# A sequence kernel in three stages: part of the second stage's input is loaded and scaled inside the first, and squares move from GpSimd to VectorE

## The reference, cut to what matters

```
q, k, v = x@Wq, x@Wk, x@Wv          # split into 16 heads
q, k    = rmsnorm(q)*qw, rmsnorm(k)*kw
gate    = softplus((k . u_n) / 8)
scores  = q.k/8 - (i-j)*omega_h*gate_j ; causal; softmax
x       = layernorm(x + (attn @ v) @ Wproj)
```

```
h = silu(x@w1' * s1) * (x@w2' * s2)
h = gelu(h@h1' * s3) ; h = gelu(h@h2' * s4)
x = layernorm(x + h@w3' * s5)
```

## Time and profile before

| | us |
|---|---|
| median of 3 runs | 3400.02 |
| lowest and highest run | 3398.07, 3406.59 |
| the profiled execution, its own time | 3401.34 |
| its span, first to last instruction | 3399.6 |
| TensorE busy | 3158.8 (93%) |
| VectorE, ScalarE, GpSimd busy | 1659.2, 1794.1, 1499.9 |
| mean granted TensorE clock | 0.97 of full |

### The profile page before, as it was taken

The page is one execution under the profiler, slowest core; times in us unless marked ns, Lnnn a source line. Parts: engine busy times, 40 slices in busy tenths (PEclk is TensorE's granted clock), DMA queues, the critical chain, the costliest instruction groups (busy, mean ns, idle before and its releaser), DMA issues. The chain is left out here.

```text
span 3399.6 us, 45979 instructions
## 1 busy us (share of the span) xinstructions
PE 3158.8 (93%) x15472; PEld 2456.8 (72%) x15472; DVE 1659.2 (49%) x3920; ACT 1794.1 (53%) x3057; POOL 1499.9 (44%) x1318
## 2 busy tenths in 40 slices
PE   3999999999999999999999999679999999899998
PEld 3667767767767677677677677467777778688887
DVE  6565565566565665655665666142222222232322
ACT  1576676667666766766776777532222222222222
POOL 4476676566666666666766766421111110000000
PEclk6899999999999999999999999889999999899999
DMA  2242332322432422422323323432232221312120
GB/s 76 65 92 49 73 85 46 84 68 50 95 77 61 99 61 51 100 48 67 87 46 81 76 50 85 111 110 87 87 87 87 87 87 38 107 66 75 42 71 19
DMA packets 196539, 249.12 MB, mean 73 GB/s; under 512 B 67280, under 2 KB 95056, under 8 KB 196176
## 3 DMA queue, kind: packets, MB, share of 16 engines
q1 hardware_dynamic: 196304, 246.19, 28.2%
HBM read 84.86 MB, written 43.52 MB: 38 GB/s over the span
## 5 line engine op out<-in xcount | busy, mean ns | idle before, releaser
L385 POOL TENSOR_TENSOR e_lo<-e_all,e_hi 128x512 fp32r<-128x512 f32 (+1 forms) x832 | 1032.1, 1249 | 654.6 <-ACT e_all L627 588.8
L627 ACT ACTIVATE e_all<-ps_s,bias 128x512 f32<-128x512 f32 (+3 forms) x1280 | 788.6, 623 | 168.3 <-PE ps_s L929 80.3
L814 DVE TENSOR_REDUCE maxes<-ps_m 128x1 f32<-128x512 f32 x768 | 521.2, 686 | 371.6 <-PE ps_m L907 368.8
L620 ACT ACTIVATE e_hi<-ps_s,bias 128x512 fp32r<-128x512 f32 (+1 forms) x832 | 560.1, 673 | 228.7 <-PE ps_s L927 134.1
L907 PE MATMUL ps_m<-k_ext,q_max 128*128 128x512 f32 (+3 forms) x1280 | 462.2, 382 | 54.3 <-DVE maxes L814 25.1
L926 PE MATMUL ps_s<-q_twice,k_split 128*128 128x512 f32 (+3 forms) x1280 | 478.0, 373 | 28.3 <-ACT e_all L627 23.3
L927 PE MATMUL ps_s<-q_ext,k_ext 128*128 128x512 f32 (+3 forms) x1280 | 469.9, 367 | 0.0
L960 PE MATMUL ps_v<-e_lo,v_main 128*66 128x512 f32 (+1 forms) x832 | 431.7, 519 | 17.3 <-POOL e_lo L385 17.3
L907 PEld LDWEIGHTS ps_m<-k_ext,q_max 128*128 128x128 f32 x1280 | 245.5, 192 | 202.5 <-DVE maxes L814 59.0
L811 DVE CUSTOM_DVE_ANT_0 ps_m<-ps_m,mask_row 128x128 f32<-128x128 f32 (+3 forms) x512 | 252.5, 496 | 282.3 <-PE ps_m L907 281.9
L949 PE MATMUL ps_v<-e_hi,v_main 128*66 128x512 f32 (+1 forms) x832 | 322.2, 387 | 0.0
(11 more groups left out here) (247 smaller groups left out, 6112.3 us busy)
## 6 DMA issues: line engine op xcount, KB each, us to landing
q_twice<-q_max SPq DMA_DIRECT2D x256, 128.0 KB, 2.3
yt<-y_out SPq DMA_DIRECT2D x128, 130.0 KB
k_ext<-kq_hi SPq DMA_DIRECT2D x128, 128.0 KB, 2.3
q_max<-kq_hi SPq DMA_DIRECT2D x128, 128.0 KB, 2.4
k_split<-kq_hi SPq DMA_DIRECT2D x128, 128.0 KB, 2.4
k_split<-kq_lo SPq DMA_DIRECT2D x128, 128.0 KB, 2.4
q_ext<-kq_lo SPq DMA_DIRECT2D x128, 128.0 KB, 2.4
y_in<-yt SPq DMA_DIRECT2D x128, 128.0 KB, 3.1
```

The costliest lines, as they stand in the source:

```text
L385: on.tensor_tensor(e_lo[:, i % LO_RING, off:QB], e_all[:, u_ % E_RING, off:QB], e_hi[:, i % HI_RING, off:QB].bitcast(F32), ALU.subtract).t ...
L620: nc.scalar.activation(e_hi[:, i % HI_RING, off:QB], ps_s[u_ % 2][:, off:QB], ACT.Exp, bias=by).then_inc(hi_done, 1)
L627: nc.scalar.activation(e_all[:, u_ % E_RING, off:QB], ps_s[u_ % 2][:, off:QB], ACT.Exp, bias=by).then_inc(ex_done, 1)
L814: nc.vector.tensor_reduce(maxes[:, qt, kc:kc + 1], ps_m[m % 2][:, 0:width], AX.X, ALU.max).then_inc(mx_free, 1)
```

## The change

Six edits, all in `attention` and the start of `ffn_up`:

1. A class `Kept` holds what lives in both functions. Its helper `room` gives one place in the on-chip memory (SBUF) to several tensors in turn: `stage` and `y_first` lie where `xt_hi`/`xt_lo` were, `r_first` and `x_tok` in `raw`, `wp_in` in `sq`, `y_hi` in `y_out`. The identity of `attention` is used in `ffn_up` too.
2. Steps are added to the list near its end, with waits on SP that the old tenant is done. SP: `stage` (4 pieces of w1 and w2, 512 KB each, from 3.0 heads before the end), `out weights` (Wproj, 1 MB, 2.55 before), `first y` (16 DMAs, from 2.4), `first r` (16 DMAs, from 1.4), `first x` (0.5). GpSimd: `first scale`, eight multiplications of 128x512, 0.36 to 0.15 heads before the end.
3. Squares: ScalarE's copy to `raw` now sets `pj_raw`; VectorE waits for it, multiplies the PSUM bank by `raw` (128x256: q and k of both heads for one tile of tokens) into `sq`, and only this sets `pj_free`. GpSimd squares no more. The sums are 4 per pair, each of 128x1024, right after every fourth project.
4. The last head's `sums` and `sums out` are taken out of `attention`; SP loads them at the start of `ffn_up`, VectorE takes the reciprocal after `turn_x(0)`, and SP stores it after the eighth piece of weights.
5. In `ffn_up`, `weights(c)` and the first block's y alternate: TensorE does `weights(c)`, `project_y(0, c)` for c = 0 to 7; ScalarE `y_hi`, `w_hi`; VectorE `y_lo`, `w_lo`. GpSimd no longer makes an identity, and scales y from block 1 on.
6. ScalarE loads the table of Silu ahead of `turn_x(0)`.

The diff, cut to its core:

```
+    for i in range(STAGES):
+        at(HEADS - 3.0 + 0.1 * i, "stage", i)
+    at(HEADS - 2.55, "out weights")
+    for c in range(OC):
+        at(HEADS - 2.4 + 0.1 * c, "first y", c)
+        at(HEADS - 1.4 + 0.1 * c, "first r", c)
+        at(HEADS - 0.36 + 0.03 * c, "first scale", c)
+    at(HEADS - 0.5, "first x")
...
-        for i in range(4):
-            at(t0 - 1.44 + 0.05 * i, "square", p, i)
-            at(t0 - 1.38 + 0.05 * i, "sum", p, i)
-            at(t0 - 1.22 + 0.04 * i, "square", p, i + 4)
-            at(t0 - 1.16 + 0.04 * i, "sum", p, i + 4)
+        for i in range(TT // TQ):
+            at(t0 - 1.72 + 0.030 * (TQ * i + 3) + 0.03, "sum", p, i)
...
-    steps += [("sums", HEADS - 1), ("sums out", HEADS - 1)]
...
+                if step[0] == "first scale":          # GpSimd
+                    c = step[1]
+                    if c == 0:
+                        gp.wait_ge(kept.first_load, 16 * 4 * OC)
+                    nc.gpsimd.tensor_tensor(kept.y_first[:, c, :], kept.y_first[:, c, :], kept.r_first[:, c, :], ALU.mult).then_inc(kept.first_scaled, 1)
...
-                    nc.scalar.activation(raw[:, t, :], work_bank(step)[:, 0:WCOLS], ACT.Copy).then_inc(pj_free, 1)
+                    nc.scalar.activation(raw[:, t, :], work_bank(step)[:, 0:WCOLS], ACT.Copy).then_inc(pj_raw, 1)
...
+                if step[0] == "project":              # VectorE
+                    p, t = step[1:]
+                    dve.wait_ge(pj_raw, TT * p + t + 1)
+                    nc.vector.tensor_tensor(sq[:, t % (2 * TQ), :], work_bank(step)[:, 0:CB], raw[:, t, 0:CB], ALU.mult).then_inc(pj_free, 1)
...
             def first_x(i):                           # ffn_up, ScalarE
+                for k in range(2):
+                    act.wait_ge(kept.y_out_done[k], 16 * NQB // 2 * HEADS)
                 for c in range(OC):
                     split_y(i, c)
+                    weights(c)
+                nc.scalar.preload_act_table(ACT.Silu)
                 turn_x(i)
...
             def first_x(i):                           # ffn_up, TensorE
                 for c in range(OC):
+                    weights(c)
                     project_y(i, c)
+                pe.wait_ge(wt_free, FIRST)
                 turn_x(i)
```

More of the change, by code:

```diff
@@ L77, in count_of, with __init__, sem, room @@
     return n * sum(m in modes for m in MODES) + sum(m in modes for m in MODES[:v])
+class Kept:
+    def __init__(self, nc, ctx):
+        def sem(name):
+            return ctx.enter_context(nc.semaphore(name))
+        def room(*uses):
+            for n, use in enumerate(uses):
+                with ExitStack() as short:
+                    stack = ctx if n == len(uses) - 1 else short
+                    yield [stack.enter_context(nc.sbuf_tensor(name, shape, dt)) for name, shape, dt in use]
+        (self.ident, self.sums), = room([("ident", [P, P], F32), ("sums", [P, 2, TT], F32)])
+        stage = [(f"up_stage{i}", [P, 8 * P], F32) for i in range(STAGES)]
+        first, late, (self.xt_hi, self.xt_lo) = room(
+            [*stage, ("up_y_first", [P, OC, NTOK], F32)],
+            [("up_stages", [P, STAGES, 8 * P], F32), ("p_lo", [P, OC, NTOK], F32R)],
+            [("xt_hi", [P, KC, T], F32R), ("xt_lo", [P, KC, T], F32R)])
+        *self.stage, self.y_first = first
+        self.p_lo = late[-1]
+        (self.r_first, self.x_tok, self.r_in), (self.gelu, self.x_hi, self.x_lo), (self.raw,) = room(
+            [("up_r_first", [P, OC, NTOK], F32), ("x_tok", [P, NT, C], F32), ("r_in", [P, 2, NTOK], F32)],
+            [("gelu", [P, AR, NTOK], F32), ("x_hi", [P, KC, NTOK], F32R), ("x_lo", [P, KC, NTOK], F32R)],
+            [("raw", [P, TT, WCOLS], F32)])
+        (self.wp_in,), (self.silu, self.prod), (self.sq,) = room(
+            [("wp_in", [P, OC, C], F32)],
+            [("silu", [P, 2, NTOK], F32), ("prod", [P, 2, NTOK], F32)],
+            [("sq", [P, 2 * TQ, 4 * D], F32)])
+        (self.y_hi,), (self.y_out,) = room([("y_hi", [P, 2, NTOK], F32R)], [("y_out", [P, 2, QB], F32)])
+        self.staged = [sem(f"up_staged{i}") for i in range(STAGES)]
+        self.wp_load = sem("up_wp_load")
+        self.x_load = sem("up_x_load")
+        self.first_load = sem("up_first_load")
+        self.first_scaled = sem("up_first_scaled")
+        self.y_out_done = [sem(f"y_out_done{i}") for i in range(2)]
 def attention_steps():
@@ L187, in sem @@
             return ctx.enter_context(nc.semaphore(name))
-        ident = sb("ident", [P, P])
+        ident, raw, sq, y_out, sums = kept.ident, kept.raw, kept.sq, kept.y_out, kept.sums
         ident_r = sb("ident_r", [P, P], F32R)
@@ L303, in attention @@
         sums_out = [sem(f"sums_out{i}") for i in range(2)]
-        y_out_done = [sem(f"y_out_done{i}") for i in range(2)]
+        y_out_done = kept.y_out_done
         steps = attention_steps()
@@ L1035, in ffn_up @@
         made = sem("up_made")
-        staged = [sem(f"up_staged{i}") for i in range(STAGES)]
+        staged, wp_load, x_load = kept.staged, kept.wp_load, kept.x_load
         wt_full = sem("up_wt_full")
@@ L1068, in ffn_up @@
             + [(h1_hi, h1_lo, i, False) for i in range(OC)]
-        rows = [(w, slice(4 * i * P, 4 * (i + 1) * P)) for w in (w1_w, w2_w) for i in range(2)] \
-            + [(h1_w, slice(i * P, (i + 1) * P)) for i in range(OC)]
+        rows = weight_rows(w1_w, w2_w, h1_w)
         NW = 2 * len(table)
@@ L1159, in first_x @@
             def first_x(i):
-                for m in range(OC * i, OC * (i + 1)):
+                for m in range(OC * (i - 1), OC * i):
                     gp.wait_ge(y_load[m % YR], 64 * (m // YR + 1))
@@ L1167, in body @@
                     first_x(i + 1)
-            over_blocks(gp, first_x, body)
+            over_blocks(gp, root, body)
         @block.scalar
@@ L1326, in weights @@
                 last.then_inc(wt_full, 1)
-            for r in range(FIRST):
-                weights(r)
-            pe.wait_ge(wt_free, FIRST)
             def project_y(i, c):
```

178 lines of the change are left out of this document (95 added, 83 removed).

## The result

The changed kernel takes 3411.0 us (median of 9 runs, 3406.8 to 3412.8); the kernel before, on the same chip, 3402.0 (9 runs, 3394.8 to 3407.6). The ratio is 1.0025 [1.0014, 1.0035]: 0.25% slower, less than the 0.3% that count as a difference here, and 30 us above the forecast of 3381. The profiled execution took 3411.8 us, its span is 3410.0 against 3399.6.

What follows compares the result with a forecast made beforehand. TensorE was taken as the bound, busy 3158.8 of 3399.6 us, so only its idle or low-clock stretches could give time. Terms of -22.4, -13.2, +6.5 and +10 sum to -19.1 from 3401.3: 3381 us on the median's scale, range 3366 to 3399.

Steps and rivals of the forecast that it cites:

- handover: From attention's last matmul to ffn_up's first y matmul: 5.6 us forecast in place of 28.0, so -22.4 us.
- y phase: The first block's y matmuls in ffn_up: eight rounds taking 17.2 us in place of 30.4, so -13.2 us.
- normalisation: The stretch in ffn_up between the first y and the body's first matmul: stays at 11.0 us.
- scaling on GpSimd: Eight multiplications of y in the last head's last units delay attention: +6.5 us, bounds 2 and 10.2.
- squares, first pair: At the start, PSUM banks wait for VectorE, busy with constants; `root` near 67.0 us, not 57.06: +10, bounds 8 and 13.
- squares, other 15 pairs: Squares and sums on VectorE in the later pairs: load covered, 0 us, up to 15 more or 10 less.
- loads in the last heads: In the last three heads, 38 DMAs pass through SP ahead of turned-tile steps: 0 us, at most 5.
- Rival (c): At 240 projects VectorE waits for `raw`, delaying maxima and TensorE; at 0.2 us each 48 us more, 3429; chance 0.10.
- Rival (b): TensorE's clock stays low through ffn_up's first y: eight rounds take 28.5 us in place of 17.2, 3392 us; chance 0.12.

## Why the prediction was wrong

| term | forecast, us | measured, us | from |
|---|---|---|---|
| handover | -22.4 | -21.9 | 6.1 for 28.0 |
| y phase | -13.2 | -12.9 | 17.5 for 30.4 |
| normalisation | 0 | 0.0 | 11.0 for 11.0 |
| scaling on GpSimd | +6.5 | +6.4 | heads 30 to 31; 0 when on VectorE |
| squares, first pair | +10 | +10.3 | `root` of pair 0 |
| squares, other 15 pairs | 0 | +25.0 | 1.6 in head 0, 23.4 in heads 1 to 28; 17.0 of it at two sums of each pair, 8.0 the rest |
| loads in the last heads | 0, at most 5 | +4.2 | heads 28 to 29 |
| sum | -19.1 | +11.1 | span: +10.4 |

*The step that failed* is "Squares, the other 15 pairs": **0**, bounds -10 and +15. It holds 25.0 of the 30 us; the loads hold 4.2, all else under 1. It reasoned that "VectorE is at 5.84 of 8 there with the sums in it, so its load is covered", and that a maximum held up by the wait for `raw` "has two banks and a spacing of over 1 us". The first is true and beside the point: at the third sum the same work in another order costs nothing. The second is true of the wait alone, and of wait and multiplication up to project 13. What I did not add up is the block that stands as one in front of a maximum: the wait, 0.42 us, and the sum of 1.2. At the third sum of a pair it is longer than both banks cover, and 0.60 us are lost. At the fourth a maximum stands between multiplication and sum, and 0.51 us are lost still. That is 17.0 us in 15 pairs. The sums were even priced, "0.25 us for each of 4 sums in 15 pairs, 15"; measured it is 0.28 for each of 4, all of it at two of them. So the price stood there as an upper bound and was about right; to take nothing of it was the error.

The remaining 8.0 us of this term the prediction has no price for. They lie where the clock falls inside attention, 13.6 us more at the low level than before. In the profiles this part goes from -3.9 to +3.7 us without VectorE's squares and from 0.0 to +7.8 with them, and the medians leave little of it; its cause stays open.

*Rival (c)* named this mechanism: the maximum behind the project is late and TensorE waits for `ps_m`. At 25.0 / 240 = 0.10 us per project it came out just under the 0.12 from which it was to decide. I gave it 0.10, and its price was thought of as a wait at each of 240 projects. In that form it is refuted: 13 intervals in a row cost nothing.

*The loads* were sized one by one at SP's issue (0.6 us each), which was right; what costs is what they do in the DMA engines to turned tiles issued right behind them. The bound of 5 held, the value 0 didn't: `q_max` waits of 9.0 us in all of attention speak of an average, and the room is small just there.

*The first pair* was right in its chain: the stop from 36.6 to 45.9 us, `root` 10.3 us later (67.3, forecast 67.0). That the bank sets most of it is shown by freeing it with the copy: 7.9 of head 0's 11.9 us come back.

*The handover* and *the y phase* were right within 0.5 us, the high clock included.
*Rival (b)*, the clock low through the y phase, didn't come about: matmuls every 0.12 us from 2224.68. The Trainium skill (TensorE: Matmul & The Clock Gate, HAM oscillation) describes an engine that stands through a long DMA wait between groups and starts each group cold; this y phase, whose waits between rounds are 0.16 us in the trace, does not show it. The prediction's sentence that the trace shows a fall only after the whole handover is wrong, though: the kernel before has 23.9 us at the low level in the middle of attention.

*Scaling* was right to 0.1 us. The Trainium skill (GPSIMD Engine Reference, Engine selection) would have had it on VectorE; the trace agrees on the time (6.4 us gone), and not on the price: 1.69 us each beside a working GpSimd, not the 0.75 of the earlier trace rows.

## What to carry to other kernels

On an engine that works through an order strictly, ask of each added instruction what stands right behind it and add up the whole block in front of that: wait, work, and whatever the work brings with it. Busy shares say nothing of this; here a block of a wait, 0.4 us and a sum of 1.2 us cost 15.6 us over 14 pairs in an engine that is half idle, and 2.7 after changing two places of the order. Put the instruction for which another engine waits first, and the bookkeeping behind it, one step late. Before you spread a loss evenly over all the places that look alike, compare the distances between marks that both traces share: here two places of sixteen held it, and the growth between two single profiles held a part that comes and goes with the clock. And price a big load by the small transfer issued right after it, not by its own issue.

## Unexpected in the hardware

VectorE's multiplication of two SBUF operands slows to a third beside a working GpSimd: 128x256 follow each other every 0.36 us with GpSimd idle (four in 1.43) and every 1.16 beside its multiplications (four in 4.65); 128x512 took 1.69 us in the last head. In the run with the bank freed by ScalarE, the 155 multiplications that overlap a GpSimd instruction take 0.69 us on the mean, the other 101 take 0.42. With one operand in PSUM, in the changed kernel, those that overlap one take 0.42 like the others. The Trainium skill (SBUF — State Buffer, Who interferes with whom) states that a VectorE instruction with two SBUF inputs contends with a GpSimd instruction that reads SBUF, while one with at most one SBUF input, outside its 2-port modes, doesn't; both halves agree with these numbers. So the change's choice to square bank times `raw` was worth 0.16 to 0.27 us a time, at the price of holding the bank.
